# One-hot arrays of a graph kernel, laid out in groups of four tiles with the tile innermost

## The reference

```python
edge_index = jnp.stack([src, dst])
x = layernorm(x + segment_sum(exp(-edge_weight)[:, None] * x[dst], src))          # L0
x = layernorm(x + mlp(segment sum, max and mean of edge_attr_32 over src))        # L1
x = layernorm(x + relu(gcn(relu(gcn(x)))))                                        # L2, over dst
x = layernorm(x + attention over edges, softmax by dst, then a layer norm)        # L3
```

## Time and profile before

| | |
|---|---|
| median of 3 runs | 10757.1 us (10755.75 to 10773.13) |
| the profiled execution | 10722.97 us, span 10721.2 us |
| busy in the span | POOL 6928.5 us (65%), DVE 5184.4 (48%), PE 2920.0 (27%), ACT 768.3 (7%) |
| first counting pass, first to last matmul | 21.3 to 390.1 us |
| second counting pass | 403.4 to 772.2 us |
| ranking pass, POOL's transfers | 807.5 to 2931 us |

### The profile page before, as it was taken

One profiled execution on the slowest core, in us unless ns is written; L12 is line 12 of the kernel. 1 busy time (PEld: TensorE's weight loads), 2 busy tenths in 40 slices (PEclk: granted clock), 3 DMA queues, 4 the chain that ended last, 5 costly groups with the idle time before them and its releaser, 6 DMA issues.

```text
span 10721.2 us, 73942 instructions
## 1 busy us (share of the span) xinstructions
PE 2920.0 (27%) x14214; PEld 2646.6 (25%) x14214; DVE 5184.4 (48%) x18978; ACT 768.3 (7%) x2419; POOL 6928.5 (65%) x6880
## 2 busy tenths in 40 slices
PE   9999888888600130000000200000002000000000
PEld 9998777777500130000000200000002000000000
DVE  5558777777699632222222222222224455555555
ACT  0003222222200010000000000000000000000000
POOL 0407777777700427777777577777777777777775
PEclk9995555555555565555555555555555555555555
DMA  5002222222277402222222122222221222222221
GB/s 226 12 7 77 72 72 75 72 72 75 75 272 273 144 24 54 52 52 54 52 52 54 37 53 53 52 54 52 52 54 27 60 58 61 58 61 59 59 60 37
DMA packets 541044, 766.54 MB, mean 71 GB/s; under 512 B 328408, under 2 KB 341632, under 8 KB 527600
## 3 DMA queue, kind: packets, MB, share of 16 engines
q1 hardware_dynamic: 321008, 509.44, 14.1%
q0 software_dynamic: 219904, 255.88, 11.1%
HBM read 352.03 MB, written 412.82 MB: 71 GB/s over the span
## 4 chain that ended last, share of the span: by engine, by line
POOL 62%; issue 21%; PE 9%; DVE 7%; DMA 1%; POOLq 0%; ACT 0%; DVEq 0%; SPq 0%; ACTq 0%
POOL arena_a L573 43%; POOL by_src L522 15%; PE bank L693 7%; POOL arena_a L542 3%; DVE arena_a L1096 2%; DVE arena_a L1091 2%; POOL adst_at_start L556 1%; PE bank L787 1%; PE bank L809 1%; DVE arena_b L1175 0%; DVE stat L1172 0%; DVE stat L1176 0%; DVE x L1174 0%; DVE x L1182 0%; DVE cap_blk L1053 0%
## 5 line engine op out<-in xcount | busy, mean ns | idle before, releaser
L573 POOL DMA_INDIRECT arena_a<-table_c,decay x3136 | 2968.3, 947 | 1190.5 <-issue 955.0
L1282 DVE SCALAR_TENSOR_TENSOR arena_a<-arena_a,same_dst 128x64 f32<-128x64 f32 x3134 | 893.4, 285 | 3000.3 <-DMA arena_a<-table_c,decay 2894.9
L522 POOL DMA_INDIRECT by_src<-arena_b,idx_blk x1568 | 1627.1, 1038 | 756.3 <-issue 497.4
L573 POOL DMA_INDIRECT arena_a<-table_at,decay x1568 | 1637.0, 1044 | 477.9 <-issue 477.9
L767 PE MATMUL bank<-ident,chunk_end 128*64 128x128 f32 (+2 forms) x8 | 2.7, 442 | 6147.6 <-DVEq L842 6147.6
L767 PEld LDWEIGHTS bank<-ident,chunk_end 128*64 128x64 f32 (+2 forms) x8 | 1.4, 240 | 6148.2 <-DVEq L842 6148.2
L735 PE MATMUL bank<-arena_b 98*128 98x128 f32 x3136 | 988.2, 418 | 226.0 <-DVE arena_b L992 226.0
L735 PEld LDWEIGHTS bank<-arena_b 98*128 98x128 f32 x3136 | 815.8, 310 | 277.6 <-DVE arena_b L992 277.6
L728 PE MATMUL bank<-arena_b 128*98 128x128 bf16 x1568 | 801.3, 511 | 1.6 <-ACT arena_b L654 1.0
L693 PE MATMUL bank<-arena_b 128*98 128x128 bf16 x3136 | 737.6, 415 | 16.5 <-DVE arena_b L921 16.5
L693 PEld LDWEIGHTS bank<-arena_b 128*98 128x98 bf16 x3136 | 736.8, 259 | 17.0 <-DVE arena_b L921 17.0
(11 more groups left out here) (260 smaller groups left out, 5317.7 us busy)
## 6 DMA issues: line engine op xcount, KB each, us to landing
states_src<-arena_a SPq DMA_DIRECT2D x98, 1024.0 KB, 4.8
states_c<-arena_a SPq DMA_DIRECT2D x196, 512.0 KB, 2.7
hrows<-by_src SPq DMA_DIRECT2D x98, 776.0 KB, 6.1
states_at<-arena_a SPq DMA_DIRECT2D x98, 576.0 KB, 3.3
x_at_start<-arena_a SPq DMA_DIRECT2D x7, 7168.0 KB, 48.4
arena_b<-x_at_start SPq DMA_DIRECT2D x98, 512.0 KB
arena_a<-table_c,decay POOLq DMA_INDIRECT x3136, 2.4
arena_b<-in_a SPq DMA_DIRECT2D x98, 256.0 KB, 3.5
```

Source lines behind the costliest of these rows:

```text
L522: pool.indirect_dma_start(out=by_src, out_offset=AT(ap=idx_blk[h][:, k:k + 1], axis=0), in_=rows[h][:, k, :], in_offset=None)\
L573: pool.indirect_dma_start(out=gb[r][:, k * w:(k + 1) * w], out_offset=None, in_=table[g], in_offset=AT(ap=src_i[:, n * J + k:n * J + k + 1 ...
L1282: ins = v.scalar_tensor_tensor(out=st[h][:, k * D:(k + 1) * D], in0=old, scalar=same_dst[:, e:e + 1], in1=gb[r][:, k * D:(k + 1) * D], op0 ...
```

## The change

The one-hot arrays and their tables are stored as `[g, n, t]`: g is the quad of the block (4 of them), n the digit's value, t the tile in the quad, innermost. The entries of one tile for n and n + 1 are 4 elements, 8 bytes, apart. The arrays are as large as before; the tables need one quad and are read again for every g (`in_groups`), the digits are read as rows of 4 (`spread`). PE and L992 read tile k by `one(onehot, k)`. The instructions of every engine, their number and their order are the same; only the patterns by which they read and write differ, and the two instructions that build the tables have a quarter of the elements.

```diff
-        oh_hi = [... .rearrange("p (n t) -> p n t", t=J) for h in range(2)]
-        oh_lo = [... .rearrange("p (n t) -> p n t", t=J)
+        oh_hi = [... .rearrange("p (g n t) -> p g n t", n=HIGH, t=Q)
+        oh_lo = [... .rearrange("p (g n t) -> p g n t", n=LOW, t=Q)
...
-        early = carve(arena_a, [("zeros", J * D), ("ih", J * HIGH // 2), ("il", J * LOW // 2)])
+        early = carve(arena_a, [("zeros", J * D), ("ih", Q * HIGH // 2), ("il", Q * LOW // 2)])
...
+        def in_groups(table):
+            return table.rearrange("p (g n) t -> p g n t", g=1).to_broadcast([P, J // Q, table.shape[1], Q])
+        def spread(digit, n):
+            return digit.rearrange("p (g o t) -> p g o t", o=1, t=Q).to_broadcast([P, J // Q, n, Q])
+        def one(onehot, k):
+            return onehot[:, k // Q, :, k % Q]
...
-                            last = pe.matmul(hist, oh_hi[h][:, :, k], oh_lo[h][:, :, k], start=False, stop=False)
+                            last = pe.matmul(hist, one(oh_hi[h], k), one(oh_lo[h], k), start=False, stop=False)
...
-            link(v.tensor_copy(iota_lo, bc(iota[:, 0:LOW], J)))
-            link(v.tensor_scalar(iota_hi, bc(iota[:, 0:HIGH], J), float(LOW), None, ALU.mult))
+            link(v.tensor_copy(iota_lo, bc(iota[:, 0:LOW], Q)))
+            link(v.tensor_scalar(iota_hi, bc(iota[:, 0:HIGH], Q), float(LOW), None, ALU.mult))
...
-                        v.tensor_tensor(oh_hi[h], iota_hi, bf(digits[o, "hi"][:, at], HIGH), ALU.is_equal)
-                        v.tensor_tensor(oh_lo[h], iota_lo, bf(digits[o, "lo"][:, at], LOW), ALU.is_equal)\
+                        v.tensor_tensor(oh_hi[h], in_groups(iota_hi), spread(digits[o, "hi"][:, at], HIGH), ALU.is_equal)
+                        v.tensor_tensor(oh_lo[h], in_groups(iota_lo), spread(digits[o, "lo"][:, at], LOW), ALU.is_equal)\
...
-                                                   scalar=1.0, in1=oh_lo[h][:, :, k], op0=ALU.mult, op1=ALU.mult,
+                                                   scalar=1.0, in1=one(oh_lo[h], k), op0=ALU.mult, op1=ALU.mult,
```

More of the change, by code:

```diff
@@ L258, in program @@
         oh = cut["onehot"].bitcast(bf16)
-        oh_hi = [oh[:, h * J * (LOW + HIGH):][:, :J * HIGH].rearrange("p (n t) -> p n t", t=J) for h in range(2)]
-        oh_lo = [oh[:, h * J * (LOW + HIGH) + J * HIGH:][:, :J * LOW].rearrange("p (n t) -> p n t", t=J)
+        oh_hi = [oh[:, h * J * (LOW + HIGH):][:, :J * HIGH].rearrange("p (g n t) -> p g n t", n=HIGH, t=Q)
+                 for h in range(2)]
+        oh_lo = [oh[:, h * J * (LOW + HIGH) + J * HIGH:][:, :J * LOW].rearrange("p (g n t) -> p g n t", n=LOW, t=Q)
                  for h in range(2)]
@@ L267, in program @@
         snap = [cut["snap"][0:HIGH, q * P:(q + 1) * P] for q in range(2)]
-        early = carve(arena_a, [("zeros", J * D), ("ih", J * HIGH // 2), ("il", J * LOW // 2)])
+        early = carve(arena_a, [("zeros", J * D), ("ih", Q * HIGH // 2), ("il", Q * LOW // 2)])
         zeros = early["zeros"]
-        iota_hi = early["ih"].bitcast(bf16).rearrange("p (n t) -> p n t", t=J)
-        iota_lo = early["il"].bitcast(bf16).rearrange("p (n t) -> p n t", t=J)
+        iota_hi = early["ih"].bitcast(bf16).rearrange("p (n t) -> p n t", t=Q)
+        iota_lo = early["il"].bitcast(bf16).rearrange("p (n t) -> p n t", t=Q)
+        def in_groups(table):
[4 more added lines that the diff above has]
+            return onehot[:, k // Q, :, k % Q]
         late = carve(hrows, [(f"tb{h}", J * TW) for h in range(R)])
@@ L713, in turn @@
                 q, at = k // Q % 2, slice(k % Q * P, (k % Q + 1) * P)
-                turned = pe.matmul(p_hi_t[q][:, at], oh_hi[h][:, :, k], ident_b[:, :], start=True, stop=True)
+                turned = pe.matmul(p_hi_t[q][:, at], one(oh_hi[h], k), ident_b[:, :], start=True, stop=True)
                 for n, w in enumerate(("hi", "lo")):
@@ L727, in body @@
                         pe.wait_ge(s("snap_ready"), t + 1)
-                        pe.matmul(hist, oh_hi[h][:, :, k], oh_lo[h][:, :, k], start=False, stop=True,
+                        pe.matmul(hist, one(oh_hi[h], k), one(oh_lo[h], k), start=False, stop=True,
                                   skip_group_check=True).then_inc(s("hist_added"), 1)
@@ L953, in onehots_of @@
             def onehots_of(i, h):
-                v.tensor_tensor(oh_hi[h], iota_hi, bf(digit_blk["hi"][h][:, :], HIGH), ALU.is_equal)
-                v.tensor_tensor(oh_lo[h], iota_lo, bf(digit_blk["lo"][h][:, :], LOW), ALU.is_equal)\
+                v.tensor_tensor(oh_hi[h], in_groups(iota_hi), spread(digit_blk["hi"][h][:, :], HIGH), ALU.is_equal)
+                v.tensor_tensor(oh_lo[h], in_groups(iota_lo), spread(digit_blk["lo"][h][:, :], LOW), ALU.is_equal)\
                     .then_inc(s("tile_onehots"), 1)
```

## The result

The changed kernel takes 10450.57 us (median of 3 runs, 10431.79 to 10451.6) where the kernel before takes 10757.1: a ratio of 0.9706, 95% interval 0.9687 to 0.9725 (the two medians alone give 0.9715). The forecast was 10478 us. The profiled execution of the changed kernel took 10431.79 us, 291.2 less than the one of before (10722.97; the sum said 279 less). Lines of code stand 13 lower in the changed file: L693 is now L706, L920 and L921 are L933 and L934, L522 is L535, L954 and L955 are L967 and L968, L992 is L1005, L1003 is L1016, L728 is L741.

What follows compares the result with a forecast made beforehand. PE's L693 was taken to bound the counting passes, POOL's L522 the ranking pass. The sum -310 + 34 - 3 = -279 gave 10444 us profiled; adding the 34 us difference to the median gave 10478, range 10385 to 10570.

Steps and rivals of the forecast that it cites:

- Part 1: Both counting passes: PE reads one-hot arrays at 8 bytes instead of 32; 2.18 us a block, 310 us gained.
- rival 1: PE and DVE reads: 8 bytes are as dear as 32, so no change, 10757 us; chance 0.06.
- Part 2: DVE's comparisons, now with rows of four: no change, 975 and 1218 ns.
- Part 3: POOL's x_at_start transfers in the second counting pass: one per block beside a busy DVE, 214 us, costed at nothing.
- Part 4: Ranking pass, DVE's side: quicker L992 moves L955 ahead of a POOL transfer, which then waits; cost 34 us.
- the 2080 of the forecast: Ranking pass: 98 blocks of 21.22 us, each with one transfer falling into L1003, before further collisions.
- The run-up: Before the ranking pass's first transfer: PE's quicker reading shortens 16 tiles, 3 us gained.
- 3: Counting passes: PE gains half, weight load and matmul following each other; 10559 to 10644 us, chance 0.10.
- rival 2: DVE's comparisons: rows of four lose the doubled rate, slower in counting and ranking passes; 11000 us, chance 0.05.
- Rival 4: Counting passes: PE's clock rises once not held by reads; period 2.03, gain 340, 10448 us; chance 0.17.
- Rival 5: Ranking pass: the L955 tie stays or turns, with part 1 as forecast; 10444 or 10400 us, chance 0.12.

Runs made afterwards that it cites:

- the ranking half alone: New layout (groups of four) in the ranking pass only, counting passes in the old layout, against the kernel before: 10735.88 us against 10705.15, ratio 1.0032.

## Why the prediction was right

**The bound.** That PE's reading sets the counting passes and POOL the ranking pass was right: the passes shrank with PE's reading, and the ranking half alone gained nothing (1.0032).

**Part 1** forecast 2.18 us a block and 155 us a pass; it is 2.21 and 153. Two terms of the loop were off and nearly cancelled. The distance p between matmuls was taken as 0.107 us and is 0.121: 15 x 0.014 = 0.21 us more in two blocks. The tail from the last matmul's start to DVE's next comparison was taken as 0.60 and is 233.21 - (230.96 + 15 x 0.121) = 0.43: 0.17 less. With the measured values the same formula gives 2.11 + 0.05 + 1.82 + 0.43 = 4.41 for two blocks, as measured. The value of p that fits was the other one, the estimate that two columns share an access (0.118); I had chosen by the nearest row, L716, whose operands are packed. That the pass still came out within 2 us is luck in part: with p = 0.121 alone the formula would have given 2.29 us a block. The Trainium skill, "Advanced Engine Details and Errata", section "SBUF Cachelines", counts accesses by lines of 16 bytes; the order of the prices (16 bytes like 32, 8 bytes about half) agrees with it for PE and for DVE's place operation (374 ns at 32 and 16 bytes, 285 at 8); at 4 bytes it is the clock and no longer the reading that sets PE's 0.060 to 0.109. The "Vector Engine (DVE) Microarchitecture Reference" of the Trainium skill, section 5.2, with its granule of two adjacent 4-byte words, measured there on 4-byte numbers, speaks for rival 1; L1005, which reads 2-byte numbers 8 bytes apart, fell to 285 ns, what it takes with packed numbers too (286, groups of one), and speaks against it.

**Part 2** was right: 975 and 1217 ns. **Part 3** was right in its result, wrong in its count: the x_at_start transfers of the changed kernel are not one to a block but one every 1.76 us; they take 1.71 us in the median (1.9 forecast) and end 48 us before the pass does:

```profile
L515 POOL DMA_INDIRECT x_at_start<-x,start_i x98: 971/1710/1952, 247.3 to 418.5; - x98
```

**Part 4** had the mechanism and the place right and the size wrong: +34 forecast, +18 measured. L1005 fell from 374 to 285 ns (291 forecast), L968 moved ahead, and a second long transfer of 1.71 us (1.70 forecast) stands in most blocks. Mis-sized was the number of blocks: the forecast let it happen in all 98 (98 x 0.8 = 78 us), and counted in the trace it happened in 76, with 1.71 - 0.96 = 0.75 us each, 57 us; the pass has 2141.5 - 2080 = 62 beyond the 2080 of the forecast. The first long transfer, into L1003 (now L1016), was put into all 98 blocks as well and fell into 75, and 15 requests fell into L967, which the forecast did not have. So the 2080 is itself a rough figure, and that 57 and 62 lie close is no proof of the count. The run-up gained 2 us (3 forecast).

**The sum** is 12 us off in the profiled runs (279 against 291). The other 15 us between 10478 and 10451 are the distance from profiled run to median, 34 us before and 19 after.

**The rivals.** 1, 2 and 3 did not come about; eight tiles in a group show rival 1's price at 16 bytes, and one tile shows rival 2's. Rival 4's number, 10448, is nearest to the measured time, but not for its reason: the clock did alternate between its two levels (0.78 over the pass), yet the matmuls did not follow it, as the pass at 1.00 shows, and the period was 2.21 and not 2.03. Groups of two bring both, and then the kernel is 30 us faster (one run). Rival 5's price was in the ranking pass, which lay between it and the forecast.

## What to carry to other kernels

Where a matmul's columns are read in steps, measure several steps and do not stop when the first halving gives nothing: here 32 to 16 bytes gave 2%, 16 to 8 nearly all of it, 4 bytes the rest. Look at VectorE's row length beside it: with 2 bytes, rows of one element, the counting passes lost all of it again on that engine. Where GpSimd's transfers are the bound, cut the long two-operand VectorE instructions beside them into pieces if VectorE has idle time; here this gave about 100 us for three edited instructions. And a loop that an edit does not touch can come out slower, as with four buffers: look at all stages and at the instruction queue's packets, not only at the stage that was edited.

## What the runs showed of the hardware that was not expected

- A matmul of 98 weight columns and 128 moving columns costs by the step of its operands 0.235 us (32 bytes), 0.230 (16), 0.121 (8), 0.060 at clock 1.00 and 0.109 mostly at the low level (4), 0.109 at the low level (2). At 8 bytes the full clock does not shorten it. A VectorE operation on 128 numbers with one such operand takes 374 ns at 32 and 16 bytes and 285 to 286 at 8, 4 and 2.
- In the second counting pass with four buffers, whose matmul records leave no gap, the granted clock was 0.50 for 4.2 us and then 1.00 to the end; in the first pass of the changed kernel, busy for 204.8 of 216 us, it was 0.78 in the mean, and at groups of two, busy for 138.1 of 199.9, it was 0.84.
- A GpSimd request that comes while a long two-operand VectorE instruction runs ends 0.83 us after that instruction's end, at offsets of 0.16, 0.33 and 1.06 us; one that comes at the very start (592.04) or 0.02 us after it still gets through in 0.95 to 0.96 us.
- With four buffers a loop without an edited line lost 137 us to waits that the profile can't name, with 110 more packets on the instruction queue; the cause is argued and not shown.
- The same kernel takes 10.7 ms on some chips and 12.6 ms on others; why is open.
